# GpSimd makes the second half of the scan's input in every odd state

## The reference

```python
x_proj = x @ W_x.T
dt_x, Bm, Cm = jnp.split(x_proj, [R, R + N], axis=-1)      # R = 64, N = 16 states
dt = jax.nn.softplus(dt_x @ W_dt.T + b_dt)
A = -jnp.exp(A_log)
dA = jnp.exp(jnp.einsum('bld,dn->bldn', dt, A))
dBx = jnp.einsum('bld,bln,bld->bldn', dt, Bm, x)
# over the tokens:  h = dA_t * h + dBx_t ;  y_t = sum over n of h * C_t
y = ys + x * D
```

## Time and profile before

| | us |
|---|---|
| median of 3 runs | 1864.08 |
| lowest and highest | 1861.53, 1865.01 |
| the profiled execution | 1862.95 |
| its span in the trace | 1861.2 |
| the loop over the states in it, from 776.4 to 903.4 | 127.0 |

### The profile page before, as it was taken

How to read it: one execution, slowest core, us unless ns; L and a number is a source line. 1 busy time by engine, 2 the same in 40 slices (tenths; PEclk the granted TensorE clock), 3 DMA queues, 4 the chain that set the end, 5 groups by cost and what they waited for, 6 DMA issues and landing times. The chain is left out here.

```text
span 1861.2 us, 30080 instructions
## 1 busy us (share of the span) xinstructions
PE 1564.7 (84%) x11028; PEld 1127.1 (61%) x11028; DVE 1342.1 (72%) x2272; ACT 829.4 (45%) x1290; POOL 454.1 (24%) x515
## 2 busy tenths in 40 slices
PE   6899999999799898376778779999998778889864
PEld 5678888888695565122366435687775345746631
DVE  3289999999685764799688674557676843668687
ACT  3367667776323453544334321433344312525544
POOL 2233333444150531155213102210000001324200
PEclk8999999999899997698888889999999759899985
DMA  4000000000000001000100010010001310010000
GB/s 154 28 24 20 28 28 28 28 28 15 12 1 11 4 2 44 1 0 0 41 11 2 29 76 41 2 38 12 13 22 57 113 36 32 2 61 2 2 1 23
DMA packets 18149, 49.82 MB, mean 27 GB/s; under 512 B 2035, under 2 KB 8436, under 8 KB 16886
## 3 DMA queue, kind: packets, MB, share of 16 engines
q1 hardware_dynamic: 18038, 48.31, 7.6%
HBM read 47.26 MB, written 1.05 MB: 26 GB/s over the span
## 5 line engine op out<-in xcount | busy, mean ns | idle before, releaser
L2235 DVE SCALAR_TENSOR_TENSOR arena<-psum,arena 128x1016 f32<-128x1016 f32 (+2 forms) x240 | 303.6, 1265 | 36.0 <-ACT arena L2172 30.3
L903 DVE TENSOR_REDUCE limits<-psum 128x4 f32<-128x512 f32 (+2 forms) x256 | 148.2, 620 | 82.0 <-PE psum L758 49.4
L2081 PE MATMUL psum<-ssm_XT_hi,ssm_split 128*128 128x512 f32 x640 | 194.9, 407 | 11.6 <-POOL ssm_split L2040 5.7
L871 ACT ACTIVATE PT<-psum 128x1024 f32<-128x1024 f32 x112 | 108.6, 1021 | 114.8 <-PE psum L789 114.8
L2081 PEld LDWEIGHTS psum<-ssm_XT_hi,ssm_split 128*128 128x128 f32 x640 | 116.4, 192 | 36.9 <-POOL ssm_split L2040 10.8
L2172 ACT ACTIVATE arena<-psum,arena 128x1024 f32<-128x1024 f32 x80 | 89.2, 1115 | 106.3 <-PE psum L2081 104.9
L758 PE MATMUL psum<-K,QR 32*128 32x256 f32 (+1 forms) x320 | 117.7, 443 | 6.8 <-DVE limits L903 5.5
L2039 POOL TENSOR_TENSOR ssm_split<-arena,const 128x256 fp32r<-128x256 f32 x80 | 58.5, 732 | 199.0 <-PE psum L2081 196.2
L2081 PE MATMUL psum<-ssm_XT_lo,ssm_split 128*128 128x512 f32 x320 | 100.9, 397 | 0.0
L2924 POOL TENSOR_TENSOR fed<-dtx,b_all 128x1024 f32<-128x1024 f32 x16 | 67.3, 4207 | 83.0 <-DVE state L3001 51.6
L1328 ACT ACTIVATE probs_g<-psum,negmax_g 128x128 f32<-128x128 f32 x128 | 45.3, 365 | 86.1 <-PE psum L1285 58.6
(11 more groups left out here) (484 smaller groups left out, 3760.0 us busy)
## 6 DMA issues: line engine op xcount, KB each, us to landing
expert_mask<-in_expert_masks SPq DMA_DIRECT2D x32, 256.0 KB, 2.9
arena<-in_ssm_in SPq DMA_DIRECT2D x16, 384.0 KB, 3.0
arena<-in_L_xattn SPq DMA_DIRECT2D x1, 5120.0 KB, 15.1
arena<-in_ssm_in SPq DMA_DIRECT2D x16, 256.0 KB, 3.0
arena<-in_L_ffn SPq DMA_DIRECT2D x1, 2592.0 KB, 9.0
arena<-in_L_xattn SPq DMA_DIRECT2D x2, 1280.0 KB, 10.4
arena<-in_L_ffn SPq DMA_DIRECT2D x1, 2176.0 KB, 8.8
ssm_gated<-in_ssm_z SPq DMA_DIRECT2D x4, 512.0 KB, 6.4
```

The source lines that it names most:

```text
L871: nc.scalar.activation(PT[:, u % 2, 2 * k:2 * k + 2, :, :].rearrange("p r h q -> p (r h q)"), p.psum[:, (2 + 2 * k) * 512:(4 + 2 * k) * 51 ...
L903: ins = nc.vector.tensor_reduce(limits[:, u % 2, r, :, k], score_bank(r)[:, :].rearrange("p (h k) -> p h k", h=4)[:, :, lo:hi], AX.X, ALU. ...
L2081: ins = nc.tensor.matmul(bank[tile_bank(r, tile) + half][:, :], w_part(tile, kw, c), x_part(kx, c, slice(half * 512, (half + 1) * 512)), s ...
L2235: ins = nc.vector.scalar_tensor_tensor(out[:, :, ago:], product[:, :, :P - ago], tap, out[:, :, ago:], ALU.mult, ALU.add)
```

## The change

GpSimd gets a second product in odd states, behind its first, with a new semaphore `second_ready`. VectorE makes `fed[:, 1]` in even states alone, and the wait of the c = 1 scan is for `fed_ready` in even states and for `second_ready` in odd ones. The wait for `state_ready.at(n * 2 + -1)`, the c = 1 scan of the state before, moves with the product. Nothing is changed on TensorE and ScalarE.

```diff
@@ gpsimd
                         pool.wait_ge(s.state_ready.sem, s.state_ready.at(n * 2 + -2))
                         nc.gpsimd.tensor_tensor(fed[:, 0, :], dtx[:, 0, :], b_all[:, r, :], ALU.mult).then_inc(s.input_ready.up(trips), 1)
+                        if r == 1:
+                            pool.wait_ge(s.state_ready.sem, s.state_ready.at(n * 2 + -1))
+                            nc.gpsimd.tensor_tensor(fed[:, 1, :], dtx[:, 1, :], b_all[:, r, :], ALU.mult).then_inc(s.second_ready.up(trips), 1)
@@ vector
                     for r in range(2):
                         n = i * 2 + r
-                        dve.wait_ge(s.b_ready.sem, s.b_ready.at(n))
-
-                        dve.wait_ge(s.state_ready.sem, s.state_ready.at(n * 2 + -1))
-                        nc.vector.tensor_tensor(fed[:, 1, :], dtx[:, 1, :], b_all[:, r, :], ALU.mult).then_inc(s.fed_ready.up(trips), 1)
+                        if r == 0:
+                            dve.wait_ge(s.b_ready.sem, s.b_ready.at(n))
+
+                            dve.wait_ge(s.state_ready.sem, s.state_ready.at(n * 2 + -1))
+                            nc.vector.tensor_tensor(fed[:, 1, :], dtx[:, 1, :], b_all[:, r, :], ALU.mult).then_inc(s.fed_ready.up(trips), 1)
                         for c in range(DC):
                             dve.wait_ge(s.decay_ready.sem, s.decay_ready.at(n * 2 + c))
                             if c == 0:
                                 dve.wait_ge(s.input_ready.sem, s.input_ready.at(n))
+                            elif r == 0:
+                                dve.wait_ge(s.fed_ready.sem, s.fed_ready.at(i))
                             else:
-                                dve.wait_ge(s.fed_ready.sem, s.fed_ready.at(n))
+                                dve.wait_ge(s.second_ready.sem, s.second_ready.at(i))
```

More of the change, by code:

```diff
@@ L290 @@
     "probs_ready", "probsT_psum", "probsT_ready", "pv_done", "operands_ready", "out_ready", "y_ready",
-    "moments_ready", "deviation_ready", "bias_added", "fed_ready", "query_weights", "key_weights", "ternary_ready", "onehot_ready", "counts_ready", "x16_ready", "perm_ready", "diag_ready", "index_ready", "sorted_ready", "sorted_out_act", "sorted_out_dve", "pos_psum", "pos_ready", "perm_turned", "sum_split", "sum_cleared", "slots_ready", "xq_ready", "hby_ready", "v_ready", "angle_ready", "const_loaded", "wo_loaded", "rest_loaded", "first_loaded", "relu_ready", "terms_ready", "term_product", "factor_ready", "shift_ready", "x_odd_ready", "x_ready", "xT_psum", "oT_psum", "oT_ready", "stored",
+    "moments_ready", "deviation_ready", "bias_added", "second_ready", "fed_ready", "query_weights", "key_weights", "ternary_ready", "onehot_ready", "counts_ready", "x16_ready", "perm_ready", "diag_ready", "index_ready", "sorted_ready", "sorted_out_act", "sorted_out_dve", "pos_psum", "pos_ready", "perm_turned", "sum_split", "sum_cleared", "slots_ready", "xq_ready", "hby_ready", "v_ready", "angle_ready", "const_loaded", "wo_loaded", "rest_loaded", "first_loaded", "relu_ready", "terms_ready", "term_product", "factor_ready", "shift_ready", "x_odd_ready", "x_ready", "xT_psum", "oT_psum", "oT_ready", "stored",
     "scaled_ready", "xqT_psum", "xqT_ready", "gu_ready", "gu_taken", "gate_scaled", "silu_ready", "hq_ready",
```

## The result

| | before | after |
|---|---|---|
| median of 5 runs, us | 1864.13 | 1872.02 |
| lowest and highest | 1861.53, 1865.47 | 1871.21, 1873.45 |
| span of the profiled execution | 1861.2 | 1871.7 |
| first scan to the end of the last read, in it | 123.15 | 131.42 |

What follows compares the result with a forecast made beforehand. VectorE, busy for 123.15 of 123.20 us, was taken to set the loop's length. Eight odd states at 1.07 us longer add 8.6: profiled 1862.95 to 1871.6, median of runs 1864.08 to 1872.7; range 1867.5 to 1880 us.

Steps and rivals of the forecast that it cites:

- VectorE's product saves 1.14 us in each of 8 states: At the odd states' c1 product: moving it off VectorE saves 1.14 us in 8 states, 9.1 us alone.
- The wait for GpSimd's c0 product is uncovered: Odd states' c0 scan: without VectorE's product ahead, it waits 0.21 us for the signal after GpSimd's first product ends.
- The second product starts first: GpSimd's second product in odd states begins at 802.35, 0.24 us ahead of the c0 scan.
- The third rival: Odd states: second product starts late, VectorE's c0 scan wins, then the c1 scan is held off; +26 us, 1890; 5%.
- It holds the scan off until 804.73, and 2.14 us of the scan are left: Odd c0 scan: blocked until the 2.38 us second product ends at 804.73, then runs 2.14 us to 806.87.
- 1.07 us for each odd state, 8.6 in all: Each odd state's net: 1.14 saved against 0.21 signal and some 2.0 held; 1.07 longer, 8.6 us over 8 states.
- The next c0 product stays behind the c1 scan: GpSimd's c0 product of the next even state starts 0.08 us after the odd c0 scan; even period stays 7.76.
- B, C, decays and the clock at nothing: TensorE's spreads of B and C, ScalarE's decays and TensorE's clock add no time in or behind the loop.
- the upper end: Top of the range, 1880 us: allows 5.2 us if the matmuls behind the last read fell at the low clock.
- (a): Odd states: the engines slow each other without holding off; +0.55 us each, 4.4 in all, 1868.5; 6%.
- (b): Odd c0 scan is not held off, only GpSimd is; c1 scan 0.78 us earlier, 6.2 gained, 1857.9; 7%.

Runs made afterwards that it cites:

- run 2: Kernel after, with GpSimd's second product in odd states replaced by a one-column product and a memset of zeros; loop 115.04 us, total 1854.49.
- Run 1: Kernel after, with GpSimd's second product in odd states covering 512 of the 1024 tokens, the rest not made; loop 122.77 us, total 1865.45.
- run 6: Kernel before, c1 product split in every state: 768 tokens on VectorE reading B from PSUM, 256 on GpSimd; loop 119.42 us, total 1858.08.
- run 7: Kernel before, c1 product split in every state: 768 tokens on VectorE reading B from SBUF, 256 on GpSimd; loop 127.66 us, total 1868.61.
- Run 3: Kernel after, with GpSimd's second product waiting for its own odd state's c0 scan instead of the preceding c1 scan; loop 150.70 us, total 1893.03.
- run 4: Kernel after, with GpSimd making both halves in every state and VectorE none; loop 140.68 us, total 1882.06.
- run 8: Kernel before, c1 product split in every state: 704 tokens on VectorE reading B from PSUM, 320 on GpSimd; loop 118.56 us, total 1859.06.

## Why the prediction was right

**VectorE's product saves 1.14 us in each of 8 states.** Right: run 2, which has the saving and no hold, is 8.11 us shorter in the loop. That is 1.01 for each odd state, the 1.14 less the 0.12 of the next step.

**The wait for GpSimd's c0 product is uncovered.** Right in kind, mis-sized: 0.21 was taken, from state 0. In the kernel after the c0 product ends at 786.04 + 4.26 = 790.30 and the scan is issued at 790.42, so 0.12. The error cost nothing, because the scan is let go by the end of the second product, whenever it was issued.

**The second product starts first.** Right, by 0.16 us instead of 0.24 (790.26 against 790.42), and by 0.15 to 0.18 in all 8 odd states. The third rival hung on this lead alone.

**It holds the scan off until 804.73, and 2.14 us of the scan are left.** Right: the product took 2.34 instead of 2.38, and the scan ended 2.15 behind it. Run 1 shows that the hold has the length of the product, run 2 that GpSimd has to read for it, and runs 6 and 7 that VectorE's product is held with both operands in SBUF and not with one in PSUM; no run put an operand of the scan itself into PSUM. Here the page "SBUF — State Buffer" of the Trainium skill, section "Who interferes with whom", and the runs agree, down to its remark that a GpSimd instruction that only writes doesn't count (run 2: scans of 4.47 for two beside a memset of 0.95).

**1.07 us for each odd state, 8.6 in all.** Measured 16.55 - 15.52 = 1.03 for each, 8.27 over the loop; the missing 0.3 us lies in the product, 0.04 shorter than taken.

**The next c0 product stays behind the c1 scan.** Right: it starts at 794.83, 0.15 behind the scan at 794.68, and takes 4.26 as before.

**B, C, decays and the clock at nothing.** Right. TensorE ran a little slower, 0.81 granted over the loop against 0.84 before, beside VectorE's work. From the end of the last read to ScalarE's copy it took 909.60 - 903.38 = 6.2 us before and 921.19 - 915.09 = 6.1 after, so the 5.2 us that the upper end allowed for did not come. That bound was itself a little low: it counts 12 matmuls of 0.43 behind the last read, 5.2 us, where the same rows show 6.2 from there to the copy. The row after:

```profile
921.19 1.86 ACT L2985 COPY xy<-psum 128x2048 f32<-128x2048 f32 x1 [15.87 <-PE psum L2965]
```

**The rivals.** (a), slowing instead of holding off, asked for a second product of 3.7 us and a c0 scan of 2.28; they were 2.34 and 4.33. (b), scans not held, falls by the same row. (c) did not occur. Run 3 shows that its costly half is real and about what it costs (a loop of 150.70); that a lead of 0.16 us is all that kept the change from it is argued, not shown.

**What remains open.** The start of the loop varies by 3.4 us between executions with equal code ahead of it, and that is a part of the spread of the totals. The traces say where most of it arises. From the last of the products of line 2058 to the cast of line 2840 the kernel before took 738.0 - 494.6 = 243.4 us, the nine others 245.5 to 246.0. In the stretch from 540 to 580 us TensorE was granted 1.00 of its full clock in the former and 0.91 to 0.94 in the latter. Another 2.5 us of spread (131.0 to 133.5 at the first of those products) lies in the first 130 us. That the clock makes the difference is likely but not shown, and why it was granted differently stays open.

## What to carry to other kernels

Before moving elementwise work from VectorE to GpSimd, add up the time of every instruction that either engine runs with its operands in SBUF: the GpSimd products and the VectorE ones with two SBUF operands take turns. In this loop it is 4.40 for two scans, 1.14 for VectorE's product and 2.17 for GpSimd's, 7.71 of a period of 7.76. So there was next to no room left for the two engines together, and replacing 1.14 by 2.3 could only lengthen the loop, though GpSimd is busy for half of it and half of that is being held. As an estimate the sum is good to about 0.15 us: with the second product in every state (run 4) it gives 4.40 + 2.17 + 2.30 = 8.87 where 8.79 was measured, and for run 7, with 0.87 for VectorE's 768 tokens and 0.72 for GpSimd's 256, 8.16 where its states take 806.26 - 798.23 = 8.03. In runs 6 and 8 it comes out at 7.29 and 7.43, and VectorE's own work (7.49 and 7.42, which is also what a state takes) is what bounds the loop or nearly so. Take one operand from PSUM where it lies there anyway, and fit GpSimd's part into the time of the instructions that do so.

## What the runs showed of the hardware

The time an instruction is held off counts as busy and appears in its own duration, on either engine: a 128x1024 GpSimd product takes 2.34 us free and 4.26 behind a scan, a scan 2.28 free and 4.33 behind a product. So a VectorE that is busy for 131.13 of 131.42 us in the kernel after is no proof that it was working all that time. About 0.13 us of the held instruction is already spent when it is let go (2.15 left of 2.28 for the scan), which should make an issue up to that much too early free of cost. State 0 of run 8 fits: 0.61 us of overlap cost 0.48. A GpSimd product of one column takes 0.19 us and a memset of 1023 columns 0.95.
